# Ranks of a pair of routing chunks from nine matmuls over shifted selections, and expert loops whose VectorE copies transposed rows three tiles ahead

## The reference

```python
# layer 0: a token goes to its top 2 of 8 experts, with biases
top_vals, top_idx = jax.lax.top_k(flat_x @ W_router + b_router, 2)
router_weights = softmax over the two chosen logits, 0 elsewhere
for e in range(8):
    h = jax.nn.relu(flat_x @ W1[e] + b1[e])        # 128 -> 512
    y = h @ W2[e] + b2[e]                          # 512 -> 128
    final_output = final_output + y * w[:, None]

# layer 1: the 8192 (token, choice) rows are sorted by expert, stably,
# and cut into 8 equal chunks; chunk e goes through expert e, whoever chose it
sort_idx = jnp.argsort(topi.reshape(-1))
chunks = xf[rev].reshape(e, n * k // e, d)
h = jax.nn.gelu(jnp.einsum('ecd,edf->ecf', chunks, w1), approximate=False)
y = jnp.einsum('ecf,efd->ecd', h, w2).reshape(n * k, d) * sw[:, None]
out = jnp.zeros((n, d)).at[rev].add(y)
```

## Time and profile before

| | |
|---|---|
| median of 3 runs | 921.75 us |
| the profiled execution's own time | 925.03 us |
| its span (first to last recorded instruction) | 923.3 us |
| TensorE, matmuls | 535.6 us busy (58%), 4815 |
| VectorE | 459.1 us (50%), 1520 |
| ScalarE | 265.5 us (29%), 442 |
| GpSimd | 384.9 us (42%), 436 |
| granted TensorE clock, mean over the span | 0.743 of full speed |
| moved by DMA | 94.56 MB, 102 GB/s |

### The profile page before, as it was taken

One profiled execution on the slowest core, in us unless ns is written; L12 is line 12 of the kernel. 1 busy time (PEld: TensorE's weight loads), 2 busy tenths in 40 slices (PEclk: granted clock), 3 DMA queues, 4 the chain that ended last, 5 costly groups with the idle time before them and its releaser, 6 DMA issues.

```text
span 923.3 us, 16362 instructions
## 1 busy us (share of the span) xinstructions
PE 535.6 (58%) x4815; PEld 434.2 (47%) x4816; DVE 459.1 (50%) x1520; ACT 265.5 (29%) x442; POOL 384.9 (42%) x436
## 2 busy tenths in 40 slices
PE   2588774313069898882455566564544002999980
PEld 2256562211058777782233455443433001988870
DVE  5674686544213332234973578777785620222224
ACT  1220011201023334343511366464544100232220
POOL 5121016655115555555000245256575571555660
PEclk9786785655569999997555578577655555999995
DMA  8999999923222222211463354332114112222218
GB/s 206 247 149 171 157 149 150 131 78 99 95 58 67 68 65 65 66 55 55 112 207 111 78 146 113 86 97 48 38 42 122 36 48 62 76 73 74 70 47 278
DMA packets 108712, 94.56 MB, mean 102 GB/s; under 512 B 12344, under 2 KB 97080, under 8 KB 108584
## 3 DMA queue, kind: packets, MB, share of 16 engines
q1 hardware_dynamic: 94584, 70.04, 36.9%
q0 software_dynamic: 9840, 21.60, 8.5%
q10 hardware_dynamic: 4224, 2.10, 0.8%
HBM read 46.15 MB, written 47.45 MB: 101 GB/s over the span
## 4 chain that ended last, share of the span: by engine, by line
DVE 28%; PE 28%; issue 11%; another core or an unknown queue 11%; DMA 8%; POOL 4%; SPq 4%; ACT 3%; DVEq 2%; POOLq 0%; ACTq 0%
PE PS L698 25%; DVE work L1205 4%; DMA work<-ys 3%; DVE stats L1210 2%; DVE XN L1228 2%; DVE work L1614 2%; DVEq L1528 2%; DVE rtmp L1205 2%; DVE X L1205 2%; POOL xs L461 1%; DMA k_parts<-work 1%; DMA q_parts<-w1l 1%; DVE nwt L1221 1%; DVE work L1534 1%
## 5 line engine op out<-in xcount | busy, mean ns | idle before, releaser
L698 PE MATMUL PS<-work 128*128 128x36 f16 (+6 forms) x1376 | 109.0, 258 | 95.4 <-DVE work L1205 70.4
L472 POOL DMA_INDIRECT ys<-work x144 | 144.4, 1003 | 34.5 <-issue 34.5
L698 PE MATMUL PS<-w,work 128*128 x1152 | 145.0, 279 | 10.5 <-issue 6.4
L698 PEld LDWEIGHTS PS<-w,work 128*128 128x128 f32 x1152 | 134.2, 192 | 21.8 <-issue 20.4
L698 PEld LDWEIGHTS PS<-work 128*128 128x128 f16 (+3 forms) x1376 | 87.9, 138 | 118.4 <-issue 80.9
L1205 DVE TENSOR_TENSOR work<-PS,work 128x128 f32<-128x128 f32 (+4 forms) x130 | 51.2, 415 | 175.6 <-issue 59.8
L497 POOL TENSOR_TENSOR work<-XN,work 128x1024 f16<-128x1024 f32 x32 | 68.0, 2126 | 162.9 <-ACT work L1149 162.6
L461 POOL DMA_INDIRECT xs<-pack,adr_i x96 | 93.9, 978 | 68.7 <-ACT pack L1053 38.6
L698 PE MATMUL PS<-work,w1h 128*128 128x256 f16 x576 | 102.5, 279 | 9.9 <-DVE work L1516 8.7
L1103 ACT ACTIVATE work<-PS,b 128x256 f32<-128x256 f32 x160 | 62.7, 474 | 110.8 <-PE PS L698 96.6
L698 PE MATMUL PS<-work,w1l 128*128 128x256 f16 x288 | 80.2, 279 | 0.3 <-issue 0.3
(11 more groups left out here) (238 smaller groups left out, 840.0 us busy)
## 6 DMA issues: line engine op xcount, KB each, us to landing
xs<-zrow SPq DMA_DIRECT2D x8, 2210.0 KB
work<-xs SPq DMA_DIRECT2D x144, 65.0 KB
work<-ys SPq DMA_DIRECT2D x16, 512.0 KB, 4.4
k_parts<-work SPq DMA_DIRECT2D x24, 128.0 KB
q_parts<-w1l SPq DMA_DIRECT2D x24, 128.0 KB
w<-k_parts SPq DMA_DIRECT2D x8, 384.0 KB
work<-q_parts SPq DMA_DIRECT2D x8, 384.0 KB
work<-k_parts SPq DMA_DIRECT2D x32, 96.0 KB
```

The source lines that it names most:

```text
L472: g.indirect_dma_start(ys[l], bass.IndirectOffsetOnAxis(xin[:, q, u, :].bitcast(U32)[:, D:D + 1], 0), yrow[:, q, u, :], None).then_inc(ff[ ...
L698: return t.matmul(o, lhsT, rhs, start=start, stop=stop, skip_group_check=True)
```

## The change

Three things change.

1. *Ranks.* The eight tiles of a pair are taken at once. One matmul adds `ones` x `cum16` to all 64 columns, with `cum16` repeated; for a distance of 1 to 7 tiles, one matmul adds `ones` x the selections of the tiles that far back to the columns from that tile on (56 down to 8 columns); a last one adds `tri` x the 64 columns of selections. Nine matmuls and nine weight loads take the place of 44 and 44. The result and the waits are the same. It is the same code for both layers.

2. *VectorE's order in the expert loops, both layers.* With `AHEAD` = 3 the first three tiles are copied ahead of the loop, and then each step is `parts(q + 3)`, `result(q)`. Before, a step was `parts(q + 1)`, `result(q - 1)`: one tile was copied ahead of the loop, and the copies stood two tiles ahead of the results. The buffers and the waits of each of the two are unchanged.

3. *Numbers of the experts, layer 0's loop.* ScalarE reads its number ahead of the waits for `up` and `y`; VectorE reads its number ahead of the waits for `y`, `turn` and the stores. TensorE's reads are unchanged.

```diff
--- before.py
+++ after.py
@@ -52,6 +52,7 @@
 QK_SCALE = (float(DH) ** -0.5, 1.0)
 MASKED = -60000.0
 STORED = 32
+AHEAD = 3
 XS_LEAD = 8
 
 
@@ -802,14 +803,12 @@
                 if p >= 1:
                     pe.wait_ge(rt[l]["rank_read"], p)
                     pe.wait_ge(rt[l]["count"], p)
-                t0 = pair(p).start
-                for s in range(2 * CT_TILES):
-                    o = PS[:, BANK_RANK[l], RANK0 + s * E:RANK0 + (s + 1) * E]
-                    mm(o, ones16[:], cum16[:], stop=False)
-                    for b in range(s):
-                        mm(o, ones16[:], sel16[:, t0 + b, :], start=False, stop=False)
-                    ins = mm(o, tri16[:], sel16[:, t0 + s, :], start=False)
-                ins.then_inc(rt[l]["rank"], 1)
+                sel, n = sel16[:, pair(p), :], 2 * CT_TILES
+                o = PS[:, BANK_RANK[l], RANK0:RANK0 + n * E].rearrange("p (s e) -> p s e", e=E)
+                mm(o, ones16[:], bc(cum16[:], 1, n), stop=False)
+                for back in range(1, n):
+                    mm(o[:, back:n, :], ones16[:], sel[:, 0:n - back, :], start=False, stop=False)
+                mm(o, tri16[:], sel, start=False).then_inc(rt[l]["rank"], 1)
 
             def route_total(l):
                 pe.wait_ge(rt[l]["count"], NP)
@@ -1094,11 +1093,12 @@
                 act.wait_ge(w_late, 16 * NL)
                 def step(i, q):
                     v, m = q % 2, (i + i0) * (XS_LEAD // 2) + q // 2
+                    if l == 0:
+                        e = act.value_load(eidx_i[0:1, l, ds(i * XS_LEAD + q, 1)], min_val=0, max_val=E - 1)
                     act.wait_ge(f["up"][v], m + 1)
                     wait(act, f["y"][v], m)
                     b = 2 + 2 * v
                     if l == 0:
-                        e = act.value_load(eidx_i[0:1, l, ds(i * XS_LEAD + q, 1)], min_val=0, max_val=E - 1)
                         for c in range(FC):
                             ins = a.activation(hid[:, v, c, :], PF[:, b * 512 + c * TILE:b * 512 + (c + 1) * TILE],
                                                ACT.Relu, bias=b1[:, ds(e * FC + c, 1)], scale=1 / WSCALE)
@@ -1518,14 +1518,14 @@
 
                 def result(i, q):
                     v, m = q % 2, (i + i0) * (XS_LEAD // 2) + q // 2
+                    if l == 0:
+                        e = dve.value_load(eidx_i[0:1, l, ds(i * XS_LEAD + q, 1)], min_val=0, max_val=E - 1)
                     dve.wait_ge(f["y"][v], m + 1)
-
                     if not (isinstance(i, int) and i + i0 == 0):
                         dve.wait_ge(f["turn"][0], (i + i0 - 1) * XS_LEAD + q + 1)
                         dve.wait_ge(f["stored"][q], (i + i0) * STORED)
                     y = PS[:, 6 + v, 0:2 * D].rearrange("p (u d) -> p u d", u=2)
                     if l == 0:
-                        e = dve.value_load(eidx_i[0:1, l, ds(i * XS_LEAD + q, 1)], min_val=0, max_val=E - 1)
                         tt(yrow[:, q, :, :], y, bc(b2b[:, ds(e * D, D)], 1, 2), ALU.add).then_inc(f["biased"][0], 1)
                         dve.wait_ge(f["biased"][0], i * XS_LEAD + q + 1)
                         y = yrow[:, q, :, :]
@@ -1534,24 +1534,21 @@
                         ins = v_.tensor_scalar(yrow[:, q, u, :], y[:, u, :], w, None, ALU.mult)
                     ins.then_inc(f["yrow"][v], 1)
 
-                def round_(i, first, last):
+                def round_(i, last):
                     for q in range(XS_LEAD):
-                        if q < XS_LEAD - 1:
-                            parts(i, q + 1)
+                        if q + AHEAD < XS_LEAD:
+                            parts(i, q + AHEAD)
                         elif not last:
-                            parts(i + 1, 0)
-                        if q >= 1:
-                            result(i, q - 1)
-                        elif not first:
-                            result(i - 1, XS_LEAD - 1)
+                            parts(i + 1, q + AHEAD - XS_LEAD)
+                        result(i, q)
 
                 rounds_ = TILES[l] // XS_LEAD
-                parts(0, 0)
-                round_(0, True, False)
+                for q in range(AHEAD):
+                    parts(0, q)
+                round_(0, False)
                 with dve.Fori(1, rounds_ - 1) as i:
-                    round_(i, False, False)
-                round_(rounds_ - 1, False, True)
-                result(rounds_ - 1, XS_LEAD - 1)
+                    round_(i, False)
+                round_(rounds_ - 1, True)
 
             def combine(l, c):
                 slot, s_, value = y_slot(l, c)
```

## The result

The changed kernel takes 916.83 us (median of 20 runs, 908.31 to 924.74), the one before, beside it, 921.85 us (20 runs, 916.87 to 925.38). The ratio is 0.9944, 95% interval 0.9926 to 0.9962: 5 us faster, where 36 were forecast.

What follows compares the result with a forecast made beforehand. No engine holds the kernel; GpSimd's scatter runs stall ranks, and VectorE's late copies idle TensorE in layer 0's loop. 925.03 - 15 - 10 - 11 = 889, with the median 3.3 below: 886 us (chance 0.50), range 866 to 911.

Steps and rivals of the forecast that it cites:

- What these have in common is GpSimd: Ranks, both layers: during GpSimd's runs of 16 scatters, a long burst of TensorE instructions stalls and its signal is late.
- Second: VectorE is ready at 149.26, the signal would be there at 143.1, gain 6.6. Third: ready at 174.39, gain 6.4.: Layer 0's second and third ranks: with nine matmuls the signal comes before VectorE needs it, gaining 6.6 and 6.4 us.
- the 15 us: Layer 0's ranks: gain kept from a sum of 22 us after SyncE takes back 7; ends 3 and 22.
- 7 us for SyncE: Layer 0's ranks: key stores queue behind SyncE's zero-fill stores and hold ScalarE's key copies, taking back 7 us.
- The 10 us: Layer 1's ranks: gain kept from a sum of 12 us, as TensorE, VectorE and ScalarE take turns; ends 3 and 12.
- Rival 3: Layer 0's ranks: even a short rank's signal waits for GpSimd's run to end, only the loop gains; 911 us, chance 0.15.
- If TensorE's idle time per tile becomes that of layer 1: Layer 0's loop, copy ahead of result: idle 22.5 us shrinks to 7, gain 15, less 4 for ScalarE's late signals: 11.
- Nothing extra: Number loads ahead of the waits, layer 0's loop: ScalarE's share is in the 11 us, VectorE's hides 0.42 us at most.
- Rival 4: Expert loop: result q waits for late transposes of q+3, +40 us over 20 pairs; slower, 930 us, chance 0.06.
- Rival 1: Layer 0's loop: denser TensorE, less GpSimd pause, later signals, loop ends no faster; ranks' 25 us only, 897 us, chance 0.17.
- The rule on instruction fetch: Ranks: fetch in blocks of 256 instructions, stalls only move, the ranks' 25 us are nought; 914 us for the profiled execution.
- Rival 2: Ranks: stalls are the recording's own, the timed kernel has none to give back; 917 us, chance 0.08.

Runs made afterwards that it cites:

- hold_b2: Kernel before, but GpSimd issues the last four of 16 scatters of layer 0's pairs 0 to 2 only after VectorE read the next rank: 921.85 us, one run at 922.
- keys_q4: The whole change plus key parts in four buffers of their own, against the kernel before: ratio 0.9926 in a session at 922.

## Why the prediction was wrong

The range was 866 to 911 and the time 916.8. Faster was right, and the size was wrong by a factor of seven.

**"What these have in common is GpSimd": right as to the place.** The stages and hold_b2 show it.

**"Second: VectorE is ready at 149.26, the signal would be there at 143.1, gain 6.6. Third: ready at 174.39, gain 6.4.": the step that failed for layer 0's ranks.** The stall went with the 35 matmuls, as forecast, and the rank's signal came before VectorE needed it. But the step took it that nothing else would be late. VectorE's own signals were, by 0.46, 1.04 and 3.00 us at the second rank and by 3.65 and 1.80 at the third. From its reading of the first rank to its going on with the second VectorE took 25.1 us before and 23.3 after: 1.9 us where 6.6 stood. The third rank gave 1.7 where 6.4 stood. The fourth gave 7.8 (32.1 to 24.3 us) where 9 stood. So two of the three terms were mostly empty and one held. That 11.1 of the 15 us remained is in part luck: the forecast had taken off 7 us for SyncE, and these covered for the two.

In layer 1 the waits for the ranks went as forecast: VectorE's idle times before the third and fourth fell from 4.78 and 6.56 us to 2.35 and nought. The 10 us were 5.1 all the same; where the rest came back is open.

Rival 3, a short rank held by the run, had the size for two of layer 0's three ranks and not the mechanism: the signals came at 148.36 and 174.29, before the runs ended.

**"If TensorE's idle time per tile becomes that of layer 1": the step that failed for the loops.** It stood for 11 us of gain, and the trace has 1.2 us of loss, with 2.9 in layer 1's loop where nought stood. The copy did get out of TensorE's way. But the step left TensorE's signals as late as they were, and they came later, 16 up projections by more than 1.5 us instead of 4, and each result stands behind one more wait for them. The order alone costs 9 us at 922. With the number loads moved as well the loss in the loops is smaller (154.6 and 157.3 us in layer 0, where the order alone has 161.0). "Nothing extra" for the number loads wasn't tested at this level: doubling them costs 15 us there, moving them was worth 2.4 at 864.

Rival 4 had the place, the result behind the transposes of a later tile, and got 6 in 100 at +40 us for the loop of layer 0; the loss in the trace is 1.2. The forecast had set aside 4 of its 15 us for late signals. Rival 1, the loop ending no faster because signals come later, is what the traces show of the loops; at 897 it still had 25 us for the ranks.

**The rule on instruction fetch** that the prediction tried gave 914 for the profiled execution, which was 915.0. That is luck: it had the ranks at nought and the loops at a gain of 11, and in the traces the ranks' two stages gained 16 and the loops lost 4. In the sessions at 864 the same 44 matmuls go through without a stall at all; no row shows a block's edge.

**The largest thing that no step asked** is whether the bubbles are in the program. 60 of 922 us are not: the kernel before runs without them in other sessions. At 864 the change is worth 3 x 0.82 us of ranks and 1 to 2.4 us of number loads, and that is the whole gain there (0.9941). At 922 the ratio is the same (0.9944), and the gain is made up otherwise: the order loses there, 9 us by itself, so ranks and number loads together must gain some 14 if the three add up; the traces have 16 in the ranks' two stages. That both levels end at 5 us is then a coincidence. It was not measured directly, since no version without the new order but with the short ranks met a session at 922.

Rival 2, stalls of the recording, stays open in another form. Profiled and timed executions agree in each session (925.03 and 921.85, 865.43 and 864.75), so profiling doesn't add the stalls; but each timed execution comes with a span and clocks too, so something is recorded in all of them. The Trainium skill (NOTIFIC — the notification-queue block, Overflow: three behaviours) says that the block holds producers back rather than lose a record inside it; a place where records drain more slowly would look like this, and no run here shows it.

## What to carry to other kernels

Before pricing a bubble, ask what it would be in another session: take a second trace of the kernel before in another session, and see which bubbles are in both. Work put in front of a wait is free only if what it waits for comes on time; an order that is neutral with prompt signals cost 1% with late ones. And where a signal is late, look at the next signals behind it before counting its wait as a gain: with a shorter burst the rank came in time, and two thirds of the wait turned up at VectorE's own signals.

## What the runs showed of the hardware

- The same program had medians of 862.7 to 864.8 us in four sessions and of 921.6 to 927.2 in three, with the whole difference in the stages where GpSimd issues indirect DMAs (26.5, 21.6, 6.1 and 5.5 us of the spans 923.3 and 863.7), and none before them.
- In the sessions at 922 an engine's own signal to itself is late too: VectorE waited 3.00 us for its own addition (after), 2.32 us in `keys_q4`. At 864 a rank inside a run of 64 scatters was signalled within 0.02 us.
- At 922 signals given during a run of scatters were late by anything from 0.01 to 9.8 us (the ranks of before, after and `keys_q4`), some during the run and some after it, and delayed instructions of TensorE and VectorE started in steps of 0.70 us or twice that.
- GpSimd's pace is the same in both kinds: 0.97 us for a scatter and 0.30 us to the next.
